# The triangular inverse taken half by half on VectorE, with parts of half 0 placed between the convolution tiles

## The chip, the cores and the metric

One core of one Trainium2 chip. The time is the device time of one execution in microseconds, lower is better. Everything is fp32 or fp32r. Engines: PE (TensorE), DVE (VectorE), ACT (ScalarE), POOL (GpSimd), SP (SyncE, which issues nearly all DMAs here).

## The reference

Input x is 8 x 256 x 128. A gated feed-forward layer with ternary weights, then an attention layer, then the feed-forward layer again, each with a layer norm ahead and a residual. The attention layer, cut to what matters here (H = 4 heads of 32 channels, chunks of 32 tokens, 8 chunks for each of 8 batches):

```python
q, k, v = silu(dwconv(hs @ Wq)), silu(dwconv(hs @ Wk)), silu(dwconv(hs @ Wv))   # 4 taps
beta = sigmoid(hs @ Wb)
q, k = l2norm(q), l2norm(k); v = v * beta; kb = k * beta        # in chunks of 32
attn = where(strict, -(kb @ k.T), 0)
T = inv(eye(32) - attn)                                          # 256 matrices of 32 x 32
u, w = T @ v, T @ kb
# scan over the 8 chunks:
local = where(incl, q_i @ k_i.T, 0); u_i = u - w @ S
o_i = q_i @ S + local @ u_i;         S = S + k_i.T @ u_i
paths = [fir_3(v), fir_15(v), fir_64(v), delta_path, v]          # causal FIR filters of 3, 15, 64 taps
stats = mean, mean square, mean |.|, norm of each path, token and head
logits = gelu([hs, stats] @ gW1 + gb1) @ gW2 + gb2; probs = softmax(...)
o = rmsnorm(sum_p probs_p * paths_p) @ Wo
```

## The kernel before

The list STEPS (L27 to L103) gives one order of steps. PE, ACT and DVE each walk the same list and each carries out its own share of every step, in that order; POOL and SP have short programs of their own. PSUM is two rings of four banks, ps_a (evicted by ACT) and ps_d (evicted by DVE), and the order in the list is the order in each ring. Each engine executes strictly in order, so an instruction that waits holds back everything behind it on its engine.

The 2048 tokens are four tiles of 512 (two batches each). Half 0 is tiles 0 and 1 (batches 0 to 3), half 1 is tiles 2 and 3. The steps of the attention layer that the change touches, in their order before (att_steps, L65 to L99):

- qkv t (PE L806): the four projections of tile t with the convolution's taps folded into the weights, 39 matmuls of 128x512. ACT evicts them (L595, L598, L600) and squares q and k (L603). mean t and var t (L773, L777; ACT L528, L531, L534; DVE L965 to L971, L1067, L1069) are the layer norm of a later tile.
- sumsq t: sums of squares per head (PE L812), reciprocal roots on ACT (L608, L610), then the normalised q, k and k times beta on DVE (L1120 to L1133). Its last instruction signals dve_nrm.
- gram i (half i): for each head, 64 matmuls of 32x32 by 32x64 (PE L836), an ACT copy (L566), a DVE product with a mask (L1139).
- inverse (DVE L1143 to L1164): two transposes bring both halves' matrices to one matrix per partition and half (L1144), 31 steps of forward substitution work on both halves together, each a product (L1154) and a subtraction (L1157) on [128, 2, k, j+1] elements with k = 31 - j, and two transposes bring the result back (L1160). ACT's numbers() (L466 to L475, four small activations and two table loads) stands at this step in ACT's order.
- token 0 to 11: transposes of k, v, kb (PE L826), evicted by ACT (L620). window 0 to 15: transposes of 96-token windows of v (PE L823), evicted by ACT into vt (L614) with the window as outer loop, a destination stride of 64 elements.
- fir 0 to 15: the FIR filters as Toeplitz products (PE L850, 32 records each), evicted by ACT (L627). Their matrices come in four groups of which SBUF holds two; SP loads groups 2 and 3 (L360) when fir 3 and fir 7 are through. yy 0 to 3 (PE L862, ACT L631) need the inverse.
- turn4 (DVE L1163): two transposes of v. Statistics q = 0 to 9: sq q on ACT (L486, a square of 1024 elements), and r1, r2, r3 on DVE (L1201, L1203, L1207, a reduction of 1024 elements each; r3 reads the square). sums(q) is the three together. aq b (PE L872; DVE L1172, L1174) and bo b (PE L872; ACT L635) prepare the recurrence.
- first and rec n (PE L884; DVE L1183, L1187): the recurrence over 8 chunks of half 0, with yy 4 to 7, aq 4 to 7 and reductions between its steps, then turn (L1213), gate and logit (PE L893, L895, L902), and half 1's recurrence beside the softmax and the mixing.
- SP waits for logit 1 before it loads the second feed-forward layer's weights; ACT rounds them (L648).

## Time and profile before

| | |
|---|---|
| median of three executions | 457.12 us (455.99 to 472.33) |
| the profiled execution | 456.23 us, its span 454.5 us |
| busy share of the span | PE 83%, DVE 68%, ACT 63%, POOL 2% |
| mean granted TensorE clock | 0.902 |

The span runs from the first to the last instruction; 1.7 us of the device time lie around it. The busy share is a mean over stages with different limits, so the stage from the first convolution tile (115.6 us) to the statistics of half 0 (turn 0 at 280.4 us) is read by itself, through the chain of waits and the engines' timelines.

### The profile page before, as it was taken

How to read it: one execution, taken by the hardware profiler on the slowest of the kernel's cores; microseconds unless marked ns; L12 is line 12 of the kernel's file. 1: busy time of each engine (PE TensorE's matmuls, PEld its weight loads, DVE VectorE, ACT ScalarE, POOL GpSimd, SP SyncE). 2: the span in 40 equal slices, each digit the busy share in tenths (PEclk: the TensorE clock that was granted, in tenths of full speed). 3: DMA queues.
4: the chain of work that ended last, by engine and by line, in shares of the span. 5: the costliest groups of instructions: out<-in, count | busy, mean ns of one | idle time of the engine just before them, and what ended most of it. 6: DMA issues, size and time to landing. Idle time of an engine off the chain costs nothing.

```text
span 454.5 us, 9702 instructions
## 1 busy us (share of the span) xinstructions
PE 377.9 (83%) x4132; PEld 279.5 (61%) x4132; DVE 307.1 (68%) x461; ACT 288.2 (63%) x434; POOL 9.1 (2%) x38
## 2 busy tenths in 40 slices
PE   5599999999988976977996668936689696978996
PEld 3377776678865746855775567522256575646885
DVE  2796779547124558699979869587867696658533
ACT  4788948888267672796554317337278739457973
POOL 4000000000000010000000000000000000000000
PEclk9899999999999995698997675877689988989999
DMA  8900009200000000000700000070000000001001
GB/s 285 300 1 2 2 1 269 57 1 1 1 1 0 1 0 4 3 0 3 209 6 4 4 4 4 1 247 8 0 1 1 1 1 2 0 1 48 3 1 46
DMA packets 13428, 17.38 MB, mean 38 GB/s; under 512 B 832, under 2 KB 9024, under 8 KB 13376
## 3 DMA queue, kind: packets, MB, share of 16 engines
q1 hardware_dynamic: 13232, 16.58, 11.7%
q8 instruction: 44, 0.72, 0.7%
q14 instruction: 8, 0.07, 0.0%
q10 hardware_dynamic: 144, 0.01, 0.0%
HBM read 15.55 MB, written 1.05 MB: 37 GB/s over the span
## 4 chain that ended last, share of the span: by engine, by line
PE 48%; DVE 25%; ACT 16%; issue 4%; DMA 4%; SPq 1%; DVEq 0%; ACTq 0%
PE ps_a L708 11%; PE ps_a L709 11%; PE ps_a L806 4%; PE ps_a L850 4%; ACT arena L614 3%; DMA w_in<-in_w 2%; PE ps_a L895 2%; PE ps_a L862 2%; PE ps_d L773 2%; PE ps_a L893 2%; DVE acts L1084 2%; DVE arena L971 2%; PE ps_d L709 2%; PE ps_d L708 2%; DVE arena L965 2%
## 5 line engine op out<-in xcount | busy, mean ns | idle before, releaser
L708 PE MATMUL ps_a<-acts,w_f 128*128 128x512 f32 x256 | 103.7, 405 | 9.1 <-ACT acts L582 8.5
L709 PE MATMUL ps_a<-acts,w_f 128*128 128x512 f32 x256 | 101.7, 397 | 0.0
L708 PEld LDWEIGHTS ps_a<-acts,w_f 128*128 128x128 f32 x256 | 49.2, 192 | 22.6 <-ACT acts L582 10.2
L709 PEld LDWEIGHTS ps_a<-acts,w_f 128*128 128x128 f32 x256 | 49.2, 192 | 10.8 <-issue 0.7
L582 ACT ACTIVATE acts<-ps_a,vec 128x512 fp32r<-128x512 f32 x64 | 44.6, 697 | 0.0
L1103 DVE TENSOR_TENSOR acts<-gbuf,acts 128x512 fp32r<-128x512 f32 x32 | 21.6, 690 | 24.9 <-ACT acts L582 24.9
L806 PE MATMUL ps_a<-xnp,conv_w 128*128 128x512 f32 x156 | 38.3, 403 | 0.0
L965 DVE SCALAR_TENSOR_TENSOR arena<-ps_d,arena 128x512 f32<-128x512 f32 x16 | 11.0, 687 | 38.9 <-ACT arena L534 29.4
L1103 DVE TENSOR_TENSOR acts<-ghbuf,acts 128x512 fp32r<-128x512 f32 x32 | 21.2, 689 | 20.8 <-ACT acts L582 20.8
L806 PEld LDWEIGHTS ps_a<-xnp,conv_w 128*128 128x128 f32 x156 | 29.3, 188 | 8.3 <-issue 1.4
L579 ACT ACTIVATE gbuf<-ps_a,vec 128x512 f32<-128x512 f32 x32 | 22.3, 697 | 10.3 <-PE ps_a L709 10.0
L850 PE MATMUL ps_a<-toep,arena 96*32 96x96 f32 x512 | 23.7, 355 | 3.9 <-ACT arena L614 2.8
L579 ACT ACTIVATE ghbuf<-ps_a,vec 128x512 f32<-128x512 f32 x32 | 22.4, 699 | 7.2 <-PE ps_a L709 7.1
L486 ACT ACTIVATE arena<-arena 128x1024 f32<-128x1024 f32 x10 | 10.3, 1052 | 22.8 <-DVE arena L1190 15.1
L850 PEld LDWEIGHTS ps_a<-toep,arena 96*32 96x32 f32 x512 | 18.8, 131 | 7.4 <-ACT arena L614 3.1
L708 PE MATMUL ps_a<-xn,w_f 128*128 128x512 f32 x32 | 15.2, 475 | 7.9 <-DVE ln L966 5.2
L627 ACT ACTIVATE arena<-ps_a 128x384 f32<-128x384 f32 x16 | 13.4, 839 | 13.1 <-PE ps_a L850 13.1
L884 PE MATMUL ps_d<-arena 32*32 32x64 f32 x448 | 11.1, 240 | 9.2 <-DVE arena L1187 4.8
L836 PE MATMUL ps_d<-arena 32*32 32x64 f32 x512 | 12.6, 289 | 6.5 <-DVE arena L966 5.8
L1079 DVE SCALAR_TENSOR_TENSOR hbuf<-ps_d,vec,gbuf 128x512 f32<-128x512 f32 x16 | 11.6, 748 | 8.4 <-ACT gbuf L550 5.1
L1157 DVE TENSOR_TENSOR arena<-arena 128x62 f32<-128x62 f32 (+15 forms) x31 | 16.4, 527 | 1.1
L1154 DVE TENSOR_TENSOR arena<-arena 128x62 f32<-128x62 f32 (+15 forms) x31 | 16.3, 527 | 1.1
...
## 6 DMA issues: line engine op xcount, KB each, us to landing
...
```

The lines of the kernel that those rows point to most:

```text
L579: e.activation(gbuf[f][:, gi % 4], src[:, :], ACT.Gelu, scale=sc).then_inc(S["act_step"], 1)
L582: e.activation(acts[f][:, j % 3, 0, m], src[:, :], ACT.Gelu, scale=sc).then_inc(S["act_a"], 1)
L614: e.activation(vt[0:WIN, :, i // 8, 4 * (i % 8):4 * (i % 8) + 4].rearrange("p c w -> p w c"), bank[0:WIN, :].rearrange("p (w c) -> p w c", ...
L627: e.activation(dst, bank[:, 0:384].rearrange("p (c t f) -> p c t f", c=4, t=DH), ACT.Copy).then_inc(S["act_a"], 1)
L708: e.matmul(bank, w, hi, start=start, stop=False)
L709: return e.matmul(bank, w, lo, start=False, stop=stop)
L806: last = e.matmul(bank, conv_w[:, hw, ww], xnp[:, hx, 2 * i:2 * i + 2, o:o + L], start=n == 0, stop=n == len(todo) - 1)
L850: last = e.matmul(bank[32 * h:32 * h + 32, WIN * c4:WIN * c4 + WIN], vt[0:WIN, DH * h + 8 * grp + dl, i // 2 % 2, :], toep[0:WIN, grp % 2, ...
L965: own(e.scalar_tensor_tensor(out=half_y2, in0=bank, scalar=eps, in1=half_y2, op0=ALU.add, op1=ALU.mult))
L1103: e.tensor_tensor(acts[f][:, j % 3, 1, m], gbuf[f][:, (KT * j + m) % 4], acts[f][:, j % 3, 0, m].bitcast(F32), ALU.subtract).then_inc(S["d ...
L1154: own(e.tensor_tensor(prod, lmat[:, :, j + 1:DH, j:j + 1].to_broadcast(shape), tinv[:, :, j:j + 1, 0:j + 1].to_broadcast(shape), ALU.mult))
L1157: own(e.tensor_tensor(sub, sub, prod, ALU.subtract))
```

## The change

- The inverse is split. Each half has its own matrices lmat and tinv; substitute(g, first, last) does steps first to last of half g with the same two instructions on [128, k, j+1]. Half 0's steps 0 to 10 stand between sumsq 2 and sumsq 3, steps 11 to 14 one behind each head of gram 1, the rest behind gram 1. Half 1's steps stand in four pieces: 0 to 15 ahead of turn4, 16 to 21 and 22 to 30 among the statistics of half 0, and its last transpose just ahead of first 0.
- gram 0 stands between qkv 2 and sumsq 2. Windows 0 to 7 stand two and two behind the convolution tiles, half 0's FIR steps behind sumsq 3, between gram 1 and the tokens. The FIR goes half by half, so that groups 0 and 1 of its matrices are loaded a second time (SP, eight more DMAs).
- sumsq t stands behind tile t, no longer behind tile t + 1, for t = 0 and 1.
- The windows are evicted with four windows innermost (both sides in the order channel, window), and the FIR results in the order filter, token, channel.
- numbers() is moved on ACT to the entry of the attention layer. sums(4) moves ahead of first 0; the order of the statistics changes, so that three reductions fewer stand behind turn 0 and three more ahead of first 0.
- Buffers are placed anew. The number of PE and ACT instructions of the stage is the same but for the order; DVE has 62 more.

The diff, cut to its core:

```diff
+SPLIT = 11
...
+FIR_ORDER = (0, 1, 4, 5, 8, 9, 12, 13, 10, 11, 14, 15, 2, 3, 6, 7)
...
-    for t in range(NT):
-        s.append(("qkv", 2, t))
-        if t + 2 < NT:
-            s += [("mean", 2, t + 2), ("var", 2, t + 2)]
-        if t:
-            s.append(("sumsq", 2, t - 1))
-    s += [("sumsq", 2, NT - 1), ("gram", 2, 0), ("gram", 2, 1), ("inverse", 2, 0)]
-    s += [("token", 2, i) for i in range(12)]
-    s += [("window", 2, i) for i in range(16)]
-    s += [("fir", 2, i) for i in range(12)]
+    for t in range(2):
+        s += [("qkv", 2, t), ("mean", 2, t + 2), ("window", 2, 2 * t), ("window", 2, 2 * t + 1),
+              ("var", 2, t + 2), ("sumsq", 2, t)]
+    s += [("qkv", 2, 2), ("gram", 2, 0), ("lmat", 2, 0), ("window", 2, 4), ("window", 2, 5), ("sumsq", 2, 2),
+          ("qkv", 2, 3), ("solve", 2, 0), ("window", 2, 6), ("window", 2, 7), ("sumsq", 2, 3)]
+    fir = [("fir", 2, i) for i in FIR_ORDER]
+    s += fir[0:4] + [("gram", 2, 1), ("lmat", 2, 1), ("solve", 2, 2), ("xt", 2, 0)]
+    s += [("token", 2, i) for i in (0, 1, 4, 5, 8, 9)] + fir[4:6]
+    s += [("token", 2, i) for i in (2, 3, 6, 7, 10, 11)] + fir[6:8]
+    s += [("window", 2, i) for i in range(8, 16)]
     for k in range(4):
-        s += [("yy", 2, k), ("fir", 2, 12 + k)]
-    s += [("turn4", 2, 0), ("sq", 2, 0), ("turn4", 2, 1), ("sq", 2, 1)] + sums(0) + [("sq", 2, 2)] + sums(1)
-    s += [("sq", 2, 3), ("aq", 2, 0), ("r1", 2, 2), ("aq", 2, 1), ("r2", 2, 2), ("r3", 2, 2), ("sq", 2, 4),
-          ("aq", 2, 2), ("r1", 2, 3), ("aq", 2, 3), ("r2", 2, 3), ("r3", 2, 3)]
-    s += [("bo", 2, b) for b in range(4)] + [("sq", 2, 5)]
+        s += [("yy", 2, k), fir[8 + k]]
+    s += [("solve", 2, 3), ("solve", 2, 4), ("turn4", 2, 0), ("sq", 2, 0), ("turn4", 2, 1), ("sq", 2, 1)] + sums(0) + [("sq", 2, 2)] + sums(1)
+    s += [("sq", 2, 3), ("aq", 2, 0), fir[12], ("solve", 2, 5), ("r1", 2, 2), ("aq", 2, 1), fir[13], ("solve", 2, 6), ("r2", 2, 2), ("r3", 2, 2), ("sq", 2, 4),
+          ("aq", 2, 2), fir[14], ("r1", 2, 3), ("aq", 2, 3), fir[15], ("r2", 2, 3), ("r3", 2, 3)]
+    s += [("bo", 2, b) for b in range(4)] + [("sq", 2, 5)] + sums(4) + [("sq", 2, 6), ("xt", 2, 1)]
     ahead = [("yy", 2, k) for k in range(4, 8)] + [("aq", 2, k) for k in range(4, 8)]
-    between = {1: [("r1", 2, 4)], 2: [("r2", 2, 4)], 3: [("r3", 2, 4)], 4: [("numbers", 2, 0)] ,
-               5: [("r1", 2, 5)], 6: [("r2", 2, 5)], 7: []}
+    between = {1: [("r1", 2, 5)], 2: [("r2", 2, 5)], 3: [("r3", 2, 5)], 4: [("numbers", 2, 0)],
+               5: [("r1", 2, 6)], 6: [("r2", 2, 6)], 7: [("r3", 2, 6)]}
     s += [("first", 2, 0)]
     for n in range(1, NCH):
         s += [("rec", 2, n), ahead[n - 1]] + between[n]
-    s += [("turn3", 2, 0), ("sq", 2, 6), ("aq", 2, 7), ("bo", 2, 4), ("bo", 2, 5), ("bo", 2, 6), ("r3", 2, 5)]
-    s += sums(6) + [("turn", 2, 0), ("bo", 2, 7), ("sq", 2, 7), ("sq", 2, 8), ("first", 2, 1),
-                       ("gate", 2, 0), ("gate", 2, 1)]
+    s += [("turn3", 2, 0), ("sq", 2, 7), ("aq", 2, 7), ("bo", 2, 4), ("bo", 2, 5), ("bo", 2, 6)]
+    s += sums(7) + [("turn", 2, 0), ("bo", 2, 7), ("sq", 2, 8), ("first", 2, 1), ("gate", 2, 0), ("gate", 2, 1)]
     half = [None] + [("rec", 2, NCH + n) for n in range(1, NCH)]
-    s += sums(7) + [("r1", 2, 8), ("r2", 2, 8), half[1], ("logit", 2, 0), ("r3", 2, 8), half[2], ("logit", 2, 1),
-                    ("lturn", 2, 0), half[3], ("soft", 2, 0), ("round", 2, 0), half[4], ("prob", 2, 0), ("mul", 2, 0), half[5], ("addmix", 2, 0), ("mul", 2, 1), ("add", 2, 1), ("osq", 2, 1),
-          half[6], ("rms", 2, 0), half[7], ("scale", 2, 0), ("turn3", 2, 1), ("sq", 2, 9), ("wo", 2, 0), ("wo", 2, 1)]
+    s += sums(8) + [half[1], ("logit", 2, 0), half[2], ("logit", 2, 1),
+                    ("lturn", 2, 0), half[3], ("soft", 2, 0), ("round", 2, 0), half[4], ("prob", 2, 0), ("mul", 2, 0),
+                    half[5], ("addmix", 2, 0), ("mul", 2, 1), ("add", 2, 1), ("osq", 2, 1),
+                    half[6], ("rms", 2, 0), half[7], ("scale", 2, 0), ("turn3", 2, 1), ("sq", 2, 9), ("wo", 2, 0), ("wo", 2, 1)]
     s += sums(9)
...
-STATS = ((4, 0), (0, 0), (1, 0), (2, 0), (4, 1), (0, 1), (3, 0), (1, 1), (2, 1), (3, 1))
-LAST_STAT = (6, 9)
+STATS = ((4, 0), (0, 0), (1, 0), (2, 0), (4, 1), (0, 1), (1, 1), (3, 0), (2, 1), (3, 1))
+LAST_STAT = (7, 9)
...
-          vk=0, bo=0, yu=4096, lmat=4096, tinv=6144, tmp=38400, ssb=22016, alt=8192, vt=14336, aq1=19968, xt=30720, paths=24576,
+          vk=0, bo=0, yu=4096, lmat0=32768, tinv0=33792, lmat1=6144, tinv1=7168, ssb=22016, alt=8192, vt0=24576, vt1=16384, aq1=19968, xt=14336, paths=24576,
...
-        lmat, tinv = at("lmat", G, DH, DH), at("tinv", G, DH, DH)
-        tmp = at("tmp", 512)
-        pall = at("paths", P, G, DH, DH)
+        lmat, tinv = ([at(f"{name}{g}", DH, DH) for g in range(G)] for name in ("lmat", "tinv"))
+        tmp = [at("xt", G, DH * DH)[:, g, 0:256] for g in range(G)]
+        pall = at("paths", G, P, DH, DH)[:, ::-1].rearrange("p g a t c -> p a g t c")
...
-            for grp in (2, 3):
-                e.wait_ge(S["pe_a"], A_AT[("fir", 2, 4 * (grp - 2) + 3)] + 1)
+            for grp, last_use in ((2, 1), (3, 5), (0, 11), (1, 15)):
+                e.wait_ge(S["pe_a"], A_AT[("fir", 2, last_use)] + 1)
...
+            e.wait_ge(S["dve_xn"], VAR_AT[("var", 2, NT - 1)] + 1)
+            own(e.memset(at("tinv0", DH * DH), 0.0))
+            e.memset(at("tinv0", DH * DH)[:, 0:DH * DH:DH + 1], 1.0).then_inc(S["eye_done"], 1)
             e.wait_ge(S["pe_a"], A_AT[("qkv", 2, NT - 1)] + 4)
-            own(e.memset(at("tinv", G * DH * DH), 0.0))
-            e.memset(at("tinv", G, DH * DH)[:, :, 0:DH * DH:DH + 1], 1.0).then_inc(S["eye_done"], 1)
+            own(e.memset(at("tinv1", DH * DH), 0.0))
+            e.memset(at("tinv1", DH * DH)[:, 0:DH * DH:DH + 1], 1.0).then_inc(S["eye_done"], 1)
...
                 if s in ENTRY:
+                    numbers()
...
-                    e.wait_ge(S["dve_nrm"], NT)
+                    e.wait_ge(S["dve_nrm"], NT * (i + 1) // 2)
...
-                        e.activation(vt[0:WIN, :, i // 8, 4 * (i % 8):4 * (i % 8) + 4].rearrange("p c w -> p w c"),
-                                     bank[0:WIN, :].rearrange("p (w c) -> p w c", w=4), ACT.Copy
+                        e.activation(vt[i // 8][0:WIN, :, 4 * (i % 8):4 * (i % 8) + 4],
+                                     bank[0:WIN, :].rearrange("p (w c) -> p c w", w=4), ACT.Copy
...
-                    dst = pall[:, 0:3, i // 2 % 2, :, c:c + 4][:, :, ::-1, :].rearrange("p f t c -> p c t f")
-                    e.activation(dst, bank[:, 0:384].rearrange("p (c t f) -> p c t f", c=4, t=DH), ACT.Copy
+                    dst = pall[:, 0:3, i // 2 % 2, :, c:c + 4][:, :, ::-1, :]
+                    e.activation(dst, bank[:, 0:384].rearrange("p (c t f) -> p f t c", c=4, t=DH), ACT.Copy
...
-                        e.wait_ge(S["act_a"], A_AT[("qkv", 2, NT - 1)] + 3)
+                    if s == ("window", 2, 0):
                         e.wait_ge(S["pad_zero"], 1)
+                    if kind == "window" and i % 4 == 0:
+                        e.wait_ge(S["act_a"], A_AT[("qkv", 2, i // 4)] + 3)
...
-                    grp = i // 4
-                    if i == 0:
-                        e.wait_ge(S["act_a"], A_AT[("window", 2, 15)] + 1)
-                    if i % 4 == 0:
-                        e.wait_ge(S[f"ld_t{grp % 2}"], 64 * (grp // 2 + 1))
+                    grp, half = i // 4, i // 2 % 2
+                    if i == FIR_ORDER[8 * half]:
+                        e.wait_ge(S["act_a"], A_AT[("window", 2, 8 * half + 7)] + 1)
+                    if i % 2 == 0:
+                        e.wait_ge(S[f"ld_t{grp % 2}"], 64 * (3 - grp // 2 if half else 1 + grp // 2))
...
+            def substitute(g, first, last):
+
+                for j in range(first, last):
+                    k = DH - 1 - j
+                    shape = [128, k, j + 1]
+                    sub = tinv[g][:, j + 1:DH, 0:j + 1]
+                    prod = tmp[g][:, 0:k * (j + 1)].rearrange("p (i c) -> p i c", i=k)
+                    settle()
+                    own(e.tensor_tensor(prod, lmat[g][:, j + 1:DH, j:j + 1].to_broadcast(shape),
+                                        tinv[g][:, j:j + 1, 0:j + 1].to_broadcast(shape), ALU.mult))
+                    settle()
+                    own(e.tensor_tensor(sub, sub, prod, ALU.subtract))
+                if last == DH - 1:
+                    settle()
...
+                        if i:
+                            substitute(0, SPLIT + h, SPLIT + h + 1)
+                elif kind == "lmat":
+                    own(e.transpose(lmat[i].rearrange("p i j -> p (i j)"),
+                                    alt[i][:, :, :, 0, :].rearrange("p h n t -> p t (h n)")))
+                elif kind == "solve":
+                    if i == 0:
+                        e.wait_ge(S["eye_done"], 1)
+                        substitute(0, 0, SPLIT)
+                    elif i == 2:
+                        substitute(0, SPLIT + H, DH - 1)
+                    else:
+                        if i == 3:
+                            e.wait_ge(S["eye_done"], 2)
+                        substitute(1, *((0, 8), (8, 16), (16, 22), (22, DH - 1))[i - 3])
+                elif kind == "xt":
+                    e.transpose(xt[:, i].rearrange("p h n t -> p t (h n)"), tinv[i].rearrange("p i j -> p (i j)")
+                                ).then_inc(S["inv_done"], 1)
...
-                        e.wait_ge(S["act_a"], A_AT[("fir", 2, 15)] + 1)
+                        e.wait_ge(S["act_a"], A_AT[("fir", 2, FIR_ORDER[8 * g + 7])] + 1)
```

## Rows read from the trace of the kernel before

**Rows 1.** The page: busy time of the engines, and their share of the chain.
```profile
PE 377.9 (83%) x4132; PEld 279.5 (61%) x4132; DVE 307.1 (68%) x461; ACT 288.2 (63%) x434; POOL 9.1 (2%) x38
PE 48%; DVE 25%; ACT 16%; issue 4%; DMA 4%; SPq 1%; DVEq 0%; ACTq 0%
```
**Rows 2.** The chain of waits, 178 to 256 us: start, length, engine and line.
```profile
177.48 0.70 DVE arena L1133
...
186.08 1.28 ACT L472
...
189.19 5.86 ACT arena L620 x12
195.05 14.25 ACT arena L614 x16
...
217.18 4.68 DMA toep<-in_fir
...
244.33 0.29 DVE arena L1172
```
**Rows 3.** DVE's timeline: start, length, line, output<-input, count, idle time before.
```profile
225.08 4.07 DVE L1160 STREAM_TRANSPOSE arena<-arena 128x1024 f32<-128x1024 f32 x2
229.02 4.04 DVE L1163 STREAM_TRANSPOSE arena<-arena 128x1024 f32<-128x1024 f32 x2
239.73 1.22 DVE L1207 TENSOR_REDUCE arena<-arena 128x32 f32<-128x1024 f32 x1 [4.45 <-ACT arena L486]
240.87 1.21 DVE L1201 TENSOR_REDUCE arena<-arena 128x32 f32<-128x1024 f32 x1
253.38 0.30 DVE L1178 STREAM_TRANSPOSE arena<-arena 128x128 f32<-128x128 f32 x1
280.36 1.95 DVE L1213 STREAM_TRANSPOSE arena<-arena 128x1024 f32<-128x1024 f32 x1 [0.61 <-ACT arena L643]
291.98 0.42 DVE L1183 TENSOR_TENSOR arena<-arena,ps_d 128x256 f32<-128x256 f32 x1 [3.75 <-PE ps_d L884]
```
**Rows 4.** DVE's timeline: one head of gram 1, two sizes of the inverse's instructions.
```profile
182.91 0.42 DVE L1139 TENSOR_TENSOR arena<-ps_d,mask 128x256 f32<-128x256 f32 x1 [0.83 <-ACT arena L566]
192.26 0.39 DVE L1154 TENSOR_TENSOR arena<-arena 128x224 f32<-128x224 f32 x1
192.69 0.40 DVE L1157 TENSOR_TENSOR arena<-arena 128x224 f32<-128x224 f32 x1
207.00 0.69 DVE L1154 TENSOR_TENSOR arena<-arena 128x512 f32<-128x512 f32 x1
207.73 0.69 DVE L1157 TENSOR_TENSOR arena<-arena 128x512 f32<-128x512 f32 x1
```
**Rows 5.** Busy time by stretch: length, PE, PEld, DVE, ACT, POOL, then PE's granted clock.
```profile
170.00:175.00 5.00, 1.81 (x85) 1.46 (x80) 4.86 (x10) 1.24 (x3) 0.00 (x0) 0.66 0.02 5
253.38:280.36 26.98, 20.07 (x934) 18.45 (x938) 20.11 (x42) 8.12 (x13) 0.00 (x0) 0.69 0.02 4
```
**Rows 6.** PE's timeline: a convolution tile, a norm, gram 0's first head.
```profile
115.58 9.29 PE L806 MATMUL ps_a<-xnp,conv_w 128*128 128x512 f32 x39
127.08 1.13 PE L777 MATMUL ps_d<-arena,mean_w 128*128 128x512 f32 x2 [1.35 <-ACT arena L528]
169.02 1.09 PE L836 MATMUL ps_d<-arena 32*32 32x64 f32 x64 [2.61 <-DVE arena L966]
```
**Rows 7.** Timelines of ACT and DVE in the convolution stage.
```profile
118.66 1.28 ACT L600 ACT_TABLE_LOAD   x1 [5.23 <-PE ps_a L806]
142.15 0.69 DVE L965 SCALAR_TENSOR_TENSOR arena<-ps_d,arena 128x512 f32<-128x512 f32 x1 [9.11 <-ACT arena L534]
145.26 0.42 DVE L1120 TENSOR_SCALAR arena<-arena 128x512 f32<-128x512 f32 x1
150.44 0.69 DVE L1133 TENSOR_TENSOR arena<-arena 128x512 f32<-128x512 f32 x1
```
**Rows 8.** The chain of waits behind turn 0: the gate's first and last matmuls.
```profile
282.36 1.65 PE ps_a L893 x3
...
289.77 0.69 PE ps_a L893 x3
```

More of the change, by code:

```diff
@@ L216, in program @@
         acts.append(sb("acts1", [128, 3, 2, KT, TILE], F32R, c3))
-        sb("small1", [128, AO["vt"] - AO["small"]], F32, c3)
+        sb("small1", [128, AO["xt"] - AO["small"]], F32, c3)
         w_f.append(sb("w_f1", [128, 5632], F32R, c3))
@@ L240, in ln_bufs @@
             if f == 1:
-                v = at("paths", P, 2, 2, TILE)
-                return {k: v[:, 1 + i, 0] for i, k in enumerate(("xc", "sq", "y", "u"))}
+                v = at("paths", G, P, 2, TILE)
+                return {k: v[:, 1, 1 + i] for i, k in enumerate(("xc", "sq", "y", "u"))}
             v = {0: ln_0, 2: at("ln", 8, TILE)}[f]
@@ L253, in program @@
         vpad = at("vpad", B, HIST + L)
-        vt = at("vt", 128, G, 32)
-        alt = at("alt", G, H, NCH, 3, DH)
+        vt = [at(f"vt{g}", 128, 32) for g in range(G)]
+        alt = [at("alt", G, H, NCH, 3, DH)[:, 1 - g] for g in range(G)]
         xt = at("xt", G, H, NCH, DH)
@@ L562, in _ @@
                 elif kind == "gram":
[L563 removed]
+                    e.wait_ge(S["dve_nrm"], NT * (i + 1) // 2)
                     for h in range(H):
                         e.wait_ge(S["pe_d"], dd + h + 1)
[L566 removed]
+                        e.activation(alt[i][:, h, :, 0], ps_d[:, (dd + h) % NRING].rearrange(
                             "p (n a t) -> p n a t", n=NCH, a=2)[:, :, 0], ACT.Copy).then_inc(S["act_l"], 1)
[L568 to L569 removed]
                 elif kind in ("hid1", "hid2"):
```

38 lines of the change are left out of this document (7 added, 31 removed).

## The prediction

> **What bounds the kernel now.** I read the page first: PE is busy 83% of the span and holds 48% of the chain, DVE 68% and 25% [rows 1]. These are means over stages, so the second view is the chain of waits, cut at the stage that the change rearranges. From 178.2 us, where DVE ends the last normalisation, it goes over gram to ACT's numbers(), the token evictions (5.86 us), the window evictions (14.25 us for 16, 0.89 each), FIR products with a wait for their matrices (4.68 us), and reaches DVE at 239.7 us [rows 2]. So before 239.7 us ACT and PE bound the stage, and the change takes their work away from there.
>
> The third view, DVE's own timeline, qualifies this. The inverse's 62 instructions run from 190.26 to 225.08 us, then two pairs of transposes, and DVE idles only 4.45 us before 239.73 us [rows 3]. From there it works without a break up to the first step of the recurrence at 253.38 us. **So a second chain, on DVE alone, lies 4.45 us below the first.** All the time taken from ACT and PE beyond this is slack, and what DVE is given in addition counts.
>
> **The price of halving.** An instruction on 224 elements has a pitch of 0.43 us, one on 512 of 0.73 [rows 4]: about 0.20 us fixed and 1.024 ns an element. One half's 31 steps have 5456 elements (the sum of (31 - j)(j + 1)), twice. Together before: 62 x 0.20 + 21824 x 0.001024 = 34.7 us, against 34.8 in the trace. A half alone: 12.4 + 11.2 = 23.6 us; two halves 47.1. DVE has 12.3 us more to do. By the same formula, pieces of half 0: steps 0 to 10 7.7 us, 11 to 14 3.6, 15 to 30 12.25. Of half 1: 0 to 15 12.25, 16 to 21 5.4, 22 to 30 6.0.
>
> **The convolution stage in the new order.** A tile costs PE 9.2 us, a norm's matmul 0.86, a sumsq 1.72 (a pair of matmuls of the same size), two windows 1.3, a gram head 1.09 at the full clock [rows 6]. numbers() falls into ACT's 5.23 us of idle time ahead of the first eviction [rows 7] and costs nothing: its 3.3 us fit; if they didn't, the first evictions would be late by the excess, and PE has four banks. Windows 0 to 3 partly fill PE's wait of 1.35 us before each norm. In order: qkv 0 115.6 to 124.8, then mean, windows, var and sumsq 0 to 129.7; qkv 1 to 138.9; the same again to 143.9; qkv 2 to 153.1. gram 0 needs sumsq 1's DVE part. ACT does two window evictions (1.8 us) ahead of tile 3's norm, plus a table load and two activations, to 145.7; DVE 3.1 us for the norm and 5.8 for sumsq 1 [rows 7], to 154.6. PE waits 1.5 us, then gram 0 to 159.1, windows 4 and 5 and sumsq 2 to 162.1, qkv 3 to 171.3 (before: 161.8). ACT evicts windows 4 and 5, loads its table (1.28 us), and gives the first root at 164.1; DVE finishes sumsq 2 at 168.8 and steps 0 to 10 at 176.5. sumsq 3's DVE part then takes 5.8 us, to 182.3; ACT's root for it is there at 177.4, so both bind about alike. **The stage ends at 182.3 us instead of 178.2, +4.1**, with gram 0, eight windows and eleven steps done in it. (gram's mask products and the first transposition, 3.6 us, lie in DVE's wait for ACT.)
>
> **From there to the recurrence, all on DVE.** First head of gram 1 ready 1.6 us after 182.3; four times a mask product and a step, 0.42 + 0.91 [rows 4], 5.3; transposition 1.9; steps 15 to 30 12.25; xt 0 2.05; half 1's steps 0 to 15 12.25; turn4 3.85; six reductions at 1.13 [rows 3] 6.75; aq 0 to 3 at 0.6 [rows 2] 2.4; steps 16 to 30 11.3; six reductions 6.75; sums(4), moved here, 3.4; xt 1 1.95. Sum 71.8 us, so first 0 starts at **254.1 us against 253.38, +0.7**. Before it was 75.2 us from 178.2: the idle 4.45, the four gram heads and one transposition are saved, the fixed costs and sums(4) added.
>
> What must stay below DVE for this. Half 0's FIR starts at about 175 and needs window 7; groups 2 and 3 of its matrices, asked for behind fir 1 and fir 5, are there 6.3 us later, before their use near 190. Windows 8 to 15 are evicted by about 208, yy and FIR end near 218, DVE wants them at 228. The reloads of groups 0 and 1 (eight DMAs on SP, queued behind waits for fir 11 and fir 15) land by about 225; SP has nothing else before the weights behind logit 1. The closest cover: ACT's fir evictions 14 and 15 now wait behind sq 4, so behind the third r3; bo 2 needs their bank. From that r3, ACT 1.0 + 0.85, two bo 4.4 and an eviction 0.6 make about 7.5 us, while DVE has 9.5 us before first 0. Slack 2.
>
> **The new eviction order** has no row. Windows cost 0.89 us now with every element 256 bytes from the last; tokens, in runs of 32, cost 0.49 each [rows 2]. Now they write runs of four and read PSUM at a stride. Bounds: 0.49, and 0.89 plus the same penalty again, 1.3. I take 0.89, the row of the same instruction. Windows stand twice on the path (before tile 3's norm, before sumsq 2's root); at 0.49 the stage ends up to 1.6 us sooner, at 1.3 up to 1.6 later. The FIR evictions are under cover either way.
>
> The Trainium skill (SBUF — State Buffer, "Door 1: The DMA port swizzle") says that accesses within 16 bytes go at full speed in SBUF and a crossing costs, and that PSUM has lines of 8 bytes. By its first half four fp32 windows side by side would be written near the contiguous price and the sum would be 1.6 us less; by its second half the strided PSUM read gives this back. No row here shows either for ACT.
>
> **Behind first 0.** Nine reductions lie between first 0 and turn 0 in both orders, so the 26.98 us stay. Behind turn 0 three reductions are gone (3.4 us), but there DVE idles 3.75 us waiting for PE [rows 3], so I count them at nothing; the cover is PE's gates. The sum on the profiled execution is 456.23 + 0.7 = 456.9, 0.2 below the shown median. **Predicted: 457.0 us.**
>
> **Rivals.**
> 1. Faster by the recurrence (0.22). In the 26.98 us DVE is busy 20.11, and PE's granted clock is 0.69 [rows 5]. With the first gate's three matmuls in 1.65 us at the low level (1.2 GHz) and the last's in 0.69 at the high one [rows 8], a PE that arrives at the higher clock gives 2 to 3 us back, a tighter loop 1 to 2, cheap evictions 1.6. It gives about 451.5. Against it: PE has even less to do ahead of the recurrence than before, which speaks for the same low clock.
> 2. Slower by PE's clock in the convolution stage (0.15). PE was busy 1.81 us in 170 to 175 and its clock fell to 0.66 there [rows 5], behind waits of 2.6 us [rows 6]. The new order makes PE wait 1.5 us and then run small matmuls just ahead of qkv 3. If the clock falls there, qkv 3 takes up to twice 9.2 us, and as sumsq 3 has only about 0.2 us of slack every microsecond counts from the first. Half of it gives +4.6: 461.6; the whole 466.
> 3. Slower by bo (0.08): fir 14 and 15's evictions hold bo 2 for more than the 2 us of slack, or the reload is late; first 0 comes 2 to 4 us later, 460.
> 4. The change doesn't do what it says: half 0's early steps only push sumsq 3 back. By the sum they delay it by 0.2 us, for ACT's roots are no sooner; if ACT were quicker (cheap evictions) up to 1.6 of their 7.7 us would be exposed. It cancels part of rival 1 and stays within 456 to 458.
>
> **Numbers.** The forecast with rival 4 has 0.55 (454.5 to 459.5), rivals 1 to 3 have 0.22, 0.15 and 0.08. For 8 in 10 the range takes in most of rival 1 and rivals 2 and 3 up to half a tile at the low clock: 450.5 to 463. No change can be told within 2%, 9.1 us: faster than 448 needs all of rival 1 and more (0.07), slower than 466.3 a whole tile at the low clock (0.07).
>
> **What would show it.** L1154 and L1157 as 124 instructions of 47 us together with no idle time; the last L1133 near 182; first 0 (L1178) near 254; ACT waiting for DVE rather than DVE for ACT between 205 and 254; r3 0 with no wait before it. It is wrong if PE's clock is below 1 before 170, if DVE waits for L1178's bo, or if the pitch at small sizes isn't 0.20 plus 1.024 ns an element.

## The result and the profile after

The changed kernel takes **462.73 us** (median; 462.54 to 463.2), against 456.79 for the kernel before it on the same chip: ratio **1.0144 [1.0125, 1.0164]**. It is 1.4% slower, where practically no change was forecast (457.0); the time lies at the upper end of the range, and the mechanism that put it there is not among the rivals. One execution of the kernel before ran slow (472.33 us), and the ratios leave it out. Every ratio in this document is to the kernel before on the same chip; its median there lay between 455.5 and 456.8 us, so times of different experiments are compared by their ratios. The profiled execution took 463.2 us with a span of 461.5, 7.0 us more than the span before.

The page of the kernel after, parts 1, 4 and 5 (to compare with [rows 1]):

```profile
PE 377.8 (82%) x4132; PEld 281.2 (61%) x4132; DVE 315.9 (68%) x523; ACT 277.6 (60%) x434; POOL 9.6 (2%) x40
...
PE 50%; DVE 28%; ACT 10%; issue 8%; DMA 3%; SPq 0%; DVEq 0%; ACTq 0%
...
L1060 DVE TENSOR_TENSOR arena<-arena 128x31 f32<-128x31 f32 (+15 forms) x62 | 21.3, 343 | 2.1
L1057 DVE TENSOR_TENSOR arena<-arena 128x31 f32<-128x31 f32 (+15 forms) x62 | 21.1, 341 | 1.9
```

The inverse is 124 instructions, 62 of each of two kinds. DVE's shares say little more. The place of the loss shows only in the chain of waits of the kernel after (start, length, what), which answers to [rows 2]:

```profile
153.73 2.03 PE ps_d L844 x142
155.76 1.64 issue
157.40 2.68 PE ps_d L844 x105
160.09 1.87 PE ps_a L831 x8
161.96 2.99 PE ps_d L818 x4
164.95 9.12 PE ps_a L812 x39
...
183.49 0.70 DVE arena L1156
...
184.24 4.24 PE ps_d L844 x210
188.48 4.33 issue
192.81 1.53 PE ps_d L844 x46
...
194.37 0.39 ACT arena L574
...
194.78 0.42 DVE arena L1162
```

L844 is gram (L836 before), L818 sumsq, L812 a convolution tile, L831 a window, L1156 the last product of a norm. Both grams contain an "issue" piece: PE waits for no other engine there, yet does not run. In gram 1 this lasts 4.33 us, exactly in front of the last 46 of its 256 matmuls.

DVE's timeline of the kernel after, the lines that answer to [rows 3] and [rows 4] (L1162 mask product, L1167 first transposition, L1180 xt, L1184 turn4, L1197 first 0, L1232 turn 0):

```profile
177.21 0.40 DVE L1060 TENSOR_TENSOR arena<-arena 128x231 f32<-128x231 f32 x1
...
179.38 0.69 DVE L973 SCALAR_TENSOR_TENSOR arena<-ps_d,arena 128x512 f32<-128x512 f32 x1 [0.70 <-ACT arena L616]
...
194.78 0.42 DVE L1162 TENSOR_TENSOR arena<-ps_d,mask 128x256 f32<-128x256 f32 x1 [4.84 <-ACT arena L574]
...
195.91 1.95 DVE L1167 STREAM_TRANSPOSE arena<-arena 128x1024 f32<-128x1024 f32 x1
...
210.03 2.01 DVE L1180 STREAM_TRANSPOSE arena<-arena 128x1024 f32<-128x1024 f32 x1
...
287.68 1.94 DVE L1232 STREAM_TRANSPOSE arena<-arena 128x1024 f32<-128x1024 f32 x1 [0.90 <-ACT arena L649]
...
298.88 0.42 DVE L1202 TENSOR_TENSOR arena<-arena,ps_d 128x256 f32<-128x256 f32 x1 [5.59 <-PE ps_d L892]
```

The 4.45 us of idle time ahead of a reduction [rows 3] are gone; DVE has none from 195.91 us to first 0, at 259.85. In their place it waits 4.84 us for the last head of gram 1.

The sum of the forecast, set against this trace:

```
stretch                           forecast    measured    off by
to the end of sumsq 3             182.3       184.2       +1.9
from there to the transposition     6.9        11.7       +4.8
transposition to first 0           64.9        63.94      -1.0
first 0 to turn 0                  26.98       27.83      +0.85
turn 0 to the end                 174.14      173.82      -0.3
                                                  sum     +6.3
```

With the 0.7 that the forecast itself added, these are the 7.0 us of span.

### The profile page after: what moved, and what is told of

Same layout as the page of the kernel before. It is cut to its first block, busy times and chain, and to the rows that moved or that the text cites. A ratio compares the mean times of both kernels' runs of the same rounds, so it can differ in the third digit from the quotient of the medians.

```text
span 461.5 us, 9781 instructions
## 1 busy us (share of the span) xinstructions
PE 377.8 (82%) x4132; PEld 281.2 (61%) x4132; DVE 315.9 (68%) x523; ACT 277.6 (60%) x434; POOL 9.6 (2%) x40
## 4 chain that ended last, share of the span: by engine, by line
PE 50%; DVE 28%; ACT 10%; issue 8%; DMA 3%; SPq 0%; DVEq 0%; ACTq 0%
PE ps_a L714 11%; PE ps_a L715 10%; PE ps_a L812 6%; DVE arena L1060 4%; DVE arena L1057 4%; PE ps_d L844 2%; DMA w_in<-in_w 2%; PE ps_d L714 2%; PE ps_d L715 2%; PE ps_d L779 2%; PE ps_a L903 2%; PE ps_a L901 2%; DVE acts L1107 2%; PE ps_a L880 2%; DVE hbuf L1102 1%
## 5 line engine op out<-in xcount | busy, mean ns | idle before, releaser
L812 PE MATMUL ps_a<-xnp,conv_w 128*128 128x512 f32 x156 | 38.3, 403 | 0.0
L812 PEld LDWEIGHTS ps_a<-xnp,conv_w 128*128 128x128 f32 x156 | 29.4, 188 | 8.5 <-issue 1.7
L858 PE MATMUL ps_a<-toep,arena 96*32 96x96 f32 x512 | 25.2, 355 | 1.3 <-issue 1.3
L880 PE MATMUL ps_a<-arena 32*32 32x64 f32 x512 | 11.8, 285 | 15.0 <-ACT arena L633 13.6
L1060 DVE TENSOR_TENSOR arena<-arena 128x31 f32<-128x31 f32 (+15 forms) x62 | 21.3, 343 | 2.1
L1057 DVE TENSOR_TENSOR arena<-arena 128x31 f32<-128x31 f32 (+15 forms) x62 | 21.1, 341 | 1.9
L892 PE MATMUL ps_d<-arena 32*32 32x64 f32 x448 | 11.8, 247 | 12.0 <-issue 7.0
L880 PEld LDWEIGHTS ps_a<-arena 32*32 32x32 f32 x512 | 10.7, 147 | 16.0 <-ACT arena L633 14.1
L892 PEld LDWEIGHTS ps_d<-arena 32*32 32x32 f32 x448 | 9.3, 124 | 16.1 <-issue 10.4
```

What stands on the lines that cost most here:

```text
L812: last = e.matmul(bank, conv_w[:, hw, ww], xnp[:, hx, 2 * i:2 * i + 2, o:o + L], start=n == 0, stop=n == len(todo) - 1)
L858: last = e.matmul(bank[32 * h:32 * h + 32, WIN * c4:WIN * c4 + WIN], vt[half][0:WIN, DH * h + 8 * grp + dl, :], toep[0:WIN, grp % 2, h, :, ...
L880: last = e.matmul(bank[c, 64 * n:64 * n + 64], yu[r, g, h, n, o:o + DH], alt[g][r, h, n, 1:3].rearrange("p x c -> p (x c)"), start=True, s ...
L892: last = e.matmul(bank[r, 64 * b:64 * b + 64].rearrange("p (x t) -> p x t", x=2), s_sb[r, g, b], aqs[g][r, b, n], start=True, stop=True)
L1057: own(e.tensor_tensor(prod, lmat[g][:, j + 1:DH, j:j + 1].to_broadcast(shape), tinv[g][:, j:j + 1, 0:j + 1].to_broadcast(shape), ALU.mult))
L1060: own(e.tensor_tensor(sub, sub, prod, ALU.subtract))
```

## The experiments

**Theory A:** in gram 1, PE waits for instructions to arrive from memory, and the FIR loads that the change asked for earlier (on SP, behind fir 1 and fir 5, which now run ahead of gram 1) fill the DMA engines just then. **Rival:** the 124 small DVE instructions, or the slower clock, are the cost.

The DMA queues of the kernel after, in 188 to 190 and then in 190 to 191 us (packets, MB, share of 16 engines), the last stretch before PE resumes:

```profile
q1 hardware_dynamic: 188, 0.49, 106.6%
...
q1 hardware_dynamic: 63, 0.15, 61.7%
q8 instruction: 1, 0.02, 7.9%
```

The loads fill the engines from 183 us on (93% and more), and the queue "instruction" shows no packet from 183 to 190. One comes through in the microsecond in which the loads run out, and the matmuls go on at 192.81.

### The loads put behind gram 1

```diff
             load_toep(e, 1)
+            e.wait_ge(S["pe_d"], D_AT[("gram", 2, 1)] + H)
             for grp, last_use in ((2, 1), (3, 5), (0, 11), (1, 15)):
```

> The changed kernel with one wait more: SP issues the loads of FIR groups 2 and 3 only when PE has ended gram 1. In the changed kernel PE stands still for 4.33 us in gram 1's last head while these loads fill the DMA engines. Theory A (PE's instructions come over the same DMA engines and queue behind the loads): the standstill shrinks to the 1.6 to 2.0 us of the other gaps marked as issue, the stage behind it comes 2.3 to 2.7 us sooner, and the time falls by 2 to 2.7 us to about 460.3 us, if FIR 8 doesn't then wait for its matrices on the path. Theory B (PE runs out of instructions in dense small matmuls whatever the DMA engines do): the gap stays above 4 us and the time within 0.5 us of 462.7. Theory C (the gap is a wait for DVE or ACT that the profile doesn't name): no change either.

Measured (run e1): 458.71 us, ratio 1.0065 [1.0037, 1.0093] to the kernel before. That is 0.8% below the kernel after: more than half of the loss is back. PE's timeline of this kernel:

```profile
183.54 2.78 PE L845 MATMUL ps_d<-arena 32*32 32x64 f32 x210 [1.24 <-DVE arena L1157]
188.00 1.50 PE L845 MATMUL ps_d<-arena 32*32 32x64 f32 x46 [1.69 <-issue]
...
197.28 3.02 PE L859 MATMUL ps_a<-toep,arena 96*32 96x96 f32 x64 [2.88 <-DMA toep<-in_fir]
```

The standstill stays at the same matmul, the 211th, but is 1.69 us instead of 4.33. Its instruction packet comes in 185 to 186 us, with no other transfer in flight. FIR now waits 2.88 us for its matrices, and this costs nothing: DVE has no idle time from the transposition (191.10) to first 0 (255.04). The gain, 3.6 us by the ratios, is larger than the 2 to 2.7 expected, because the stretch behaved as a whole: gram 1 from first to last matmul lasted 5.96 us here and 10.07 in the kernel after, where the first 210 also took 4.24 us instead of 2.78.

### The same loads beside gram 1, in the kernel before

```diff
+            e.wait_ge(S["ld_t0"], 64)
+            e.wait_ge(S["ld_t1"], 64)
+            e.wait_ge(S["pe_d"], D_AT[("gram", 2, 1)])
+            load_toep(e, 0)
+            load_toep(e, 1)
...
-                        e.wait_ge(S[f"ld_t{grp % 2}"], 64 * (grp // 2 + 1))
+                        e.wait_ge(S[f"ld_t{grp % 2}"], 64 * (grp // 2 + 2))
```

> The kernel before, with the FIR matrices of groups 0 and 1 loaded a second time while gram 1 runs (SP issues the eight DMAs when PE has ended gram 0; the same data, 2.3 MB). Nobody waits for these loads: the first FIR step comes 23 us later. Theory A (instructions queue behind loads): PE's standstills in gram 1 and the tokens behind it grow by 2 to 3 us in sum, gram 1 is on the path of ACT and DVE alike, and the time rises by 1.5 to 4 us, to 458 to 461 us. Theory B (no link between loads and standstills): within 0.5 us of the kernel before.

Measured (run e2): 457.75 us, ratio 1.0054 [1.0029, 1.0080], 2.5 us slower. PE's timeline of this kernel:

```profile
177.99 5.64 PE L841 MATMUL ps_d<-arena 32*32 32x64 f32 x244 [0.56 <-DVE arena L1144]
186.17 0.64 PE L841 MATMUL ps_d<-arena 32*32 32x64 f32 x12 [2.55 <-issue]
```

In the kernel before, the 256 are one piece:

```profile
179.19 6.35 PE L836 MATMUL ps_d<-arena 32*32 32x64 f32 x256 [0.56 <-DVE arena L1139]
```

With nothing else changed, eight loads beside a gram lengthen it from 6.35 to 8.82 us. The rival is out for this part: neither halving nor a new order is in this kernel, and the first 244 matmuls run as fast as before (5.64 us against 5.63 in its chain of waits). So it is shown, from both sides, that loads beside a gram lengthen it. That the matmuls wait for their instructions is an inference, from the fixed place of the standstill and the times of the instruction packets; no run took the two apart. The packet need not wait for the loads to run out: here it comes through at 183 to 184 us, with the engines still full of loads (103%), and PE resumes at 186.17.

### Gram 0 back behind the tiles

```diff
-    s += [("qkv", 2, 2), ("gram", 2, 0), ("lmat", 2, 0), ("window", 2, 4), ("window", 2, 5), ("sumsq", 2, 2),
-          ("qkv", 2, 3), ("solve", 2, 0), ("window", 2, 6), ("window", 2, 7), ("sumsq", 2, 3)]
+    s += [("qkv", 2, 2), ("window", 2, 4), ("window", 2, 5), ("sumsq", 2, 2),
+          ("qkv", 2, 3), ("window", 2, 6), ("window", 2, 7), ("sumsq", 2, 3), ("gram", 2, 0), ("lmat", 2, 0), ("solve", 2, 0)]
```

> The changed kernel with gram 0, its transposition and steps 0 to 10 placed behind sumsq 3, the windows left between the tiles. Theory (gram 0 between the tiles pays for itself by cover): qkv 3 starts 8 us sooner, sumsq 3 ends near 176.5 instead of 184.1, but the transposition and eleven steps (9.5 us) stand uncovered on DVE, so gram 1 begins to be read 2 to 4 us later and the time rises by 2 to 4 us over 462.7. Rival (the cost of gram 0 between the tiles, a standstill of 1.6 us and a matmul clock of 0.56 behind it, is larger than its cover): the time falls by 1 to 3 us.

Measured (run e4): 457.08 us, ratio 1.0042 [1.0015, 1.0069]. I had expected it slower than the kernel after; it is 1.0% faster, and my price for this step fell. sumsq 3 ends at 175.4 us instead of 184.2, and steps 0 to 10 now lie in the wait for gram 1. Its PE and DVE timelines:

```profile
181.64 2.78 PE L844 MATMUL ps_d<-arena 32*32 32x64 f32 x210
188.34 1.50 PE L844 MATMUL ps_d<-arena 32*32 32x64 f32 x46 [3.92 <-issue]
```

```profile
190.32 0.42 DVE L1162 TENSOR_TENSOR arena<-ps_d,mask 128x256 f32<-128x256 f32 x1 [0.36 <-ACT arena L574]
```

The standstill is still 3.92 us, but DVE waits only 0.36: there are eleven steps to do meanwhile.

### Both at once

```diff
+            e.wait_ge(S["pe_d"], D_AT[("gram", 2, 1)] + H)
```

(the line of the first experiment, in the kernel of the one before this)

> The run e4 (gram 0, its transposition and steps 0 to 10 behind the tiles) with the loads of groups 2 and 3 behind gram 1 as in e1. In e4 the standstill of PE in gram 1 still lasts 3.92 us, but DVE is at work on steps 0 to 10 and idles only 0.36 us for it. Theory (the standstill costs only where DVE waits for gram 1): the standstill falls to about 1.7 us and the time falls by 0 to 1 us from 457.1, against 4.0 us in e1. Rival (the loads cost time by themselves): it falls by 2.5 to 4 us as there.

Measured (run e11): 457.65 us, ratio 1.0043 [1.0023, 1.0064], no different from 1.0042. Gram 1 shrinks from 8.20 to 5.11 us:

```profile
181.52 2.78 PE L845 MATMUL ps_d<-arena 32*32 32x64 f32 x210
185.76 0.87 PE L845 MATMUL ps_d<-arena 32*32 32x64 f32 x46 [1.47 <-issue]
```

and the time does not move. So the standstill is paid only where DVE has nothing to do beside it, and the two repairs are two ways to the same 4 us, not a sum. The same numbers price gram 0's place by itself: with the loads out of the way in both, 1.0065 with it between the tiles and 1.0043 with it behind them, 0.2%, which the intervals don't tell apart.

### Without the late steps of half 1

```diff
-                        substitute(1, *((0, 8), (8, 16), (16, 22), (22, DH - 1))[i - 3])
+                        substitute(1, *((0, 8), (8, 16), (16, 16), (16, 16))[i - 3])
                 elif kind == "xt":
+                    settle()
```

> The changed kernel without steps 16 to 30 of half 1's inverse (30 DVE instructions, 11.1 us in its trace; this part of the computation is left out). If DVE alone bounds the stretch from 196 us to the recurrence, the time falls by 10 to 11.1 us, to about 452 us. If PE's or ACT's work (bo 2 and bo 3, held back by the evictions behind the fourth square, or the second load of the matrices) lies close below, it falls by less: first 0 had 4.1 us behind bo 3's eviction, which shifts with the removed instructions, so a fall of under 8 us would mean such a chain.

Measured (run e5): 450.82 us, ratio 0.9895 [0.9867, 0.9923], 2.5% (11.4 us) below the kernel after. The steps left out take 5.2 + 5.9 us there. Its first 0, on DVE's timeline:

```profile
246.26 0.28 DVE L1198 STREAM_TRANSPOSE arena<-arena 128x128 f32<-128x128 f32 x1
```

13.6 us sooner than 259.85. 2.5 of it was there at the transposition (193.43 us instead of 195.91), and 11.1 us come from the stretch, which is what the steps took. Nothing took their place: DVE bounds the stretch up to first 0, as the forecast had it.

### The light ACT work in the kernel before

numbers() at the entry and both eviction orders, without halving:

```diff
-                        e.activation(vt[0:WIN, :, i // 8, 4 * (i % 8):4 * (i % 8) + 4].rearrange("p c w -> p w c"),
-                                     bank[0:WIN, :].rearrange("p (w c) -> p w c", w=4), ACT.Copy
+                        e.activation(vt[0:WIN, :, i // 8, 4 * (i % 8):4 * (i % 8) + 4],
+                                     bank[0:WIN, :].rearrange("p (w c) -> p c w", w=4), ACT.Copy
...
-                    dst = pall[:, 0:3, i // 2 % 2, :, c:c + 4][:, :, ::-1, :].rearrange("p f t c -> p c t f")
-                    e.activation(dst, bank[:, 0:384].rearrange("p (c t f) -> p c t f", c=4, t=DH), ACT.Copy
+                    dst = pall[:, 0:3, i // 2 % 2, :, c:c + 4][:, :, ::-1, :]
+                    e.activation(dst, bank[:, 0:384].rearrange("p (c t f) -> p f t c", c=4, t=DH), ACT.Copy
```

> The kernel before with ACT's share of the change alone: numbers() at the entry of the attention layer, windows and FIR results evicted in the new element order; order of steps, joint inverse and buffers as before. My theory (a DVE chain lies 4.45 us below the ACT and PE chain): ACT's chain gets shorter by 3.1 (numbers), 16 x 0.39 = 6.2 (windows) and more (FIR), the FIR's end by about 9, DVE's idle time of 4.45 us before the third reduction goes to about 0, and nothing beyond it: 456.8 - 4.4 = 452.4 us. Rival: the ACT and PE chain was all that counted, 447 to 448 us. Rival: what is gained is given back in the recurrence, 456 to 457 us.

Measured (run e3): 456.2 us, ratio 1.0020 [0.9988, 1.0051]: no gain, and my expectation fell. Its PE timeline tells why,

```profile
214.06 5.87 PE L849 MATMUL ps_a<-toep,arena 96*32 96x96 f32 x128 [1.16 <-DMA toep<-in_fir]
226.24 1.93 PE L861 MATMUL ps_a<-arena 32*32 32x64 f32 x64 [6.31 <-DVE arena L1159]
```

and DVE's:

```profile
239.49 1.22 DVE L1206 TENSOR_REDUCE arena<-arena 128x32 f32<-128x1024 f32 x1 [5.53 <-ACT arena L486]
```

PE is through fir 11 at 219.9 us, 7.8 sooner than before, and then waits 6.31 us for the inverse's transposition, with fir 12 to 15 queued behind yy 0 to 3. The interleave of yy and FIR then takes its old time, DVE again waits 5.53 us for ACT's sq 0 (4.45 before), and all is as it was. **The two chains of the forecast were one:** inverse, transposition, yy and FIR in turn on PE, ACT's sq 0, DVE. The 4.45 us were no slack of an independent chain; they were FIR's last four groups, done where DVE could see them.

### FIR wholly ahead of yy, inverse not halved

```diff
-    s += [("fir", 2, i) for i in range(12)]
-    for k in range(4):
-        s += [("yy", 2, k), ("fir", 2, 12 + k)]
+    s += [("fir", 2, i) for i in range(16)]
+    s += [("yy", 2, k) for k in range(4)]
```

(on top of the previous experiment)

> The kernel before with ACT's lighter evictions and numbers() moved (as in the run e3), and all sixteen FIR steps ahead of yy 0. In e3 PE reached yy 0 early and waited 6.31 us for the inverse with four FIR steps queued behind it, so ACT's first square still came at 237.9 and DVE idled 5.53 us. Theory (the order on PE, inverse to yy to FIR to square to r3, holds DVE): with the FIR ahead, this idle time goes to nearly 0 and the time falls by 4.5 to 5.5 us, to about 451 us. Rival (something else holds the square): no change from e3, 456 us. Rival (given back in the recurrence): 454 to 456 us.

Measured (run e7): **450.59 us, ratio 0.9886 [0.9855, 0.9916]**, 1.1% faster than the kernel before, as expected, and the fastest complete kernel of this study. Its PE and DVE timelines:

```profile
226.62 3.77 PE L860 MATMUL ps_a<-arena 32*32 32x64 f32 x255 [1.48 <-DVE arena L1158]
```

```profile
233.99 1.22 DVE L1205 TENSOR_REDUCE arena<-arena 128x32 f32<-128x1024 f32 x1
...
247.63 0.32 DVE L1176 STREAM_TRANSPOSE arena<-arena 128x128 f32<-128x128 f32 x1
```

The FIR products lie beside the inverse, PE idles 1.48 us before yy, the first r3 (L1205) waits for nothing, and first 0 comes at 247.63 instead of 253.38. Of the 5.75 us, 4.45 are that idle time, 0.4 were there before the inverse ended, and the four transpositions behind the inverse took 0.8 less. No step of the inverse was halved for them.

### One joint inverse in the new order

All 31 steps over both halves behind gram 1, both transpositions right behind; the rest as in the kernel after:

```diff
-    s += fir[0:4] + [("gram", 2, 1), ("lmat", 2, 1), ("solve", 2, 2), ("xt", 2, 0)]
+    s += fir[0:4] + [("gram", 2, 1), ("lmat", 2, 1), ("solve", 2, 0), ("xt", 2, 0), ("xt", 2, 1)]
...
-                    shape = [128, k, j + 1]
+                    shape = [128, G, k, j + 1]
```

> The changed kernel with the inverse in one piece again: all 31 steps on both halves together behind gram 1, both transposes right behind, everything else in the changed order. 62 DVE instructions fewer; DVE's total falls by 12.3 us, but the 7.5 us of steps between the tiles and the 3.6 us between gram 1's heads were mostly under cover. Theory (the fixed 0.2 us of each added instruction, less what the cover hides): the convolution stage ends 1 to 2 us sooner (179 to 183), gram 1's path about 1.5 us shorter, then 34.8 + 4 us instead of 12.1 + 2 + 12 + 11.1 + 2, so the recurrence starts 1 to 4 us sooner and the time is 459 to 462 us. If halving itself made the change slow, it should fall to 456.8 us or below. If the small pieces are all hidden, it stays at 462.7 or rises.

Measured (run e6): 466.86 us, ratio 1.026 [1.0187, 1.0334] (four executions), slower still than the kernel after; I had expected 459 to 462, so this expectation fell too. Its PE and DVE timelines:

```profile
191.09 1.50 PE L844 MATMUL ps_d<-arena 32*32 32x64 f32 x46 [5.90 <-issue]
```

```profile
193.05 0.42 DVE L1165 TENSOR_TENSOR arena<-ps_d,mask 128x256 f32<-128x256 f32 x1 [7.13 <-ACT arena L574]
...
247.13 1.22 DVE L1220 TENSOR_REDUCE arena<-arena 128x32 f32<-128x1024 f32 x1 [7.31 <-ACT arena L493]
```

There are two waits. No steps of half 0 fill the standstill in gram 1 (7.13 us; PE's last 46 matmuls waited 5.90); yet the last head's product comes at 193.05, 1.7 us sooner than in the kernel after, as gram 0 and sumsq 2 took less. And yy, with FIR between, waits for the whole inverse (7.31 us): this one makes the kernel the slower of the two, for from the last head's product to first 0 it takes 71.8 us, the kernel after 65.1. So what halving bought was work done inside the first wait and the removal of the second, and each has another remedy.

### The joint inverse with both remedies

FIR ahead of yy (the four FIR steps among the statistics too), and the loads behind gram 1:

```diff
-    for k in range(4):
-        s += [("yy", 2, k), fir[8 + k]]
+    s += fir[8:16] + [("yy", 2, k) for k in range(4)]
...
+            e.wait_ge(S["pe_d"], D_AT[("gram", 2, 1)] + H)
```

> The run e6 (changed order, joint inverse) with all of half 1's FIR steps ahead of yy 0, and with the loads of groups 2 and 3 behind gram 1 as in e1. In e6 DVE idled 7.3 us behind the inverse, for FIR results that PE held back behind yy 0, and 7.1 us in gram 1. Theory (halving pays only because yy and FIR were interleaved, and DVE's sum decides otherwise): both idle times shrink, by about 7 and 4 us, and the time is 454 to 457 us, below the run e1 (458.7), which is the same with the inverse halved. If halving has a merit of its own, it stays above e1.

Measured (run e9): 455.84 us, ratio 1.0005 [0.9986, 1.0025], against 1.0065 for the halved kernel with late loads (e1): 0.6%, 2.7 us. That is not the price of halving: first 0 comes almost at the same time in the two profiled executions, this kernel's line first,

```profile
254.80 0.30 DVE L1191 STREAM_TRANSPOSE arena<-arena 128x128 f32<-128x128 f32 x1
```

```profile
255.04 0.27 DVE L1198 STREAM_TRANSPOSE arena<-arena 128x128 f32<-128x128 f32 x1
```

and the other 2.4 us lie behind it, where both kernels have the same steps; no run says why. Then gram 0 behind the tiles as well, and gram 1 ahead of half 0's FIR:

```diff
-    s += [("qkv", 2, 2), ("gram", 2, 0), ("lmat", 2, 0), ("window", 2, 4), ("window", 2, 5), ("sumsq", 2, 2),
-          ("qkv", 2, 3), ("window", 2, 6), ("window", 2, 7), ("sumsq", 2, 3)]
-    s += fir[0:4] + [("gram", 2, 1), ("lmat", 2, 1), ("solve", 2, 0), ("xt", 2, 0), ("xt", 2, 1)]
+    s += [("qkv", 2, 2), ("window", 2, 4), ("window", 2, 5), ("sumsq", 2, 2),
+          ("qkv", 2, 3), ("window", 2, 6), ("window", 2, 7), ("sumsq", 2, 3), ("gram", 2, 0), ("lmat", 2, 0)]
+    s += [("gram", 2, 1)] + fir[0:4] + [("lmat", 2, 1), ("solve", 2, 0), ("xt", 2, 0), ("xt", 2, 1)]
```

> The run e9 (joint inverse, half 1's FIR ahead of yy 0, loads behind gram 1) with gram 0 and its transposition behind the tiles and half 0's first four FIR steps behind gram 1. No step of the inverse is between the tiles or between the heads. sumsq 3 should end near 175.5 instead of 184, gram 1's last head near 182, the inverse begin near 185 instead of 192.4: 7 us sooner, and the time 448.5 to 450 us, at or below the run e7 (450.6). If the interleaving in the convolution stage had been worth its cost, it stays above 455.

Measured (run e10): 452.52 us, ratio 0.993 [0.9903, 0.9958], against 1.0043 for the halved kernel with both changes (e11): 1.1%, 5 us. Of these, 4.1 are there at first 0 (250.71 against 254.78). It is faster than the kernel before, but 2.5 to 4 us short of the expectation. Its PE and DVE timelines:

```profile
218.59 3.05 PE L858 MATMUL ps_a<-toep,arena 96*32 96x96 f32 x64 [5.01 <-DMA toep<-in_fir]
...
225.16 1.98 PE L870 MATMUL ps_a<-arena 32*32 32x64 f32 x124
```

```profile
233.68 1.22 DVE L1220 TENSOR_REDUCE arena<-arena 128x32 f32<-128x1024 f32 x1 [2.93 <-ACT arena L493]
```

Now the last FIR matrices are late (5.01 us), yy stands behind FIR, and DVE waits 2.93 us: the same in-order queue as before, from its other end. That is the size of what is missing, though I did not run a kernel with earlier loads to prove it.

## Why the prediction was wrong

The forecast was no change, and the kernel lost 1.4%. The step that failed is the term for gram 1, "four times a mask product and a step, 0.42 + 0.91": it let DVE be the bound there, took PE's heads at their full pace, and put what the moved loads do to PE at nothing. Measured, the stretch took 11.7 us instead of 6.9: PE stood still for 4.33 us beside these loads, and with the loads behind gram 1 (e1) it took 7.6. That 462.73 us still lies inside the range is luck: the upper end was set for rival 2, half a tile at the low clock, and that did not happen.

**What bounds the kernel (wrong).** The chain of waits was read rightly up to 239.7 us, but the second chain "4.45 us below the first" does not exist. ACT's load there is not the bound: taking it away gives 1.0020 [0.9988, 1.0051]. The idle 4.45 us come from yy and FIR sharing PE's queue, and moving four list entries, on top of the lighter ACT work, recovers them and more (the four entries moved alone were not run). This failure did not move the sum, for the 4.45 us are gone in the kernel after as forecast; it misjudged what it takes to win them.

**The price of halving (right).** Steps 0 to 10 took 7.5 us (7.7 forecast), 15 to 30 of half 0 12.1 (12.25), 0 to 15 of half 1 12.0 (12.25), 16 to 21 5.2 (5.4), 22 to 30 5.9 (6.0): 1 to 3% below 0.20 us plus 1.024 ns an element. That DVE bounds the whole stretch is shown by the run without the late steps. Against a joint inverse with FIR first the halves cost 0.2 us up to first 0 (e1 and e9), and 4.1 with gram 0 behind the tiles (e11 and e10). These pairs differ also in FIR's place, the second also in that of gram 1, so the figures are for the pair of orders, not for the 12.3 us of work alone. A halved kernel with FIR ahead of yy was not run; as DVE has no idle time in e1 from the transposition to first 0, I would expect nothing from it.

**The convolution stage, 182.3 us forecast, 184.2 measured (failed by 1.9, and in its premise).** numbers() was hidden, the windows cheaper than assumed, and steps 0 to 10 ended at 177.53, and DVE, after two short products, still waited 0.70 us for ACT's root (179.38), so they did not push sumsq 3 back: rival 4 is out. But from gram 0's start (153.73) to the end of the windows PE took 8.2 us against 5.7: a standstill of 1.64 us and matmuls at a lower clock. sumsq 2 then took 2.99 instead of 1.72. Busy time of the kernel after by stretch (length, PE, PEld, DVE, ACT, POOL, PE's granted clock, DMA share, GB/s):

```profile
155.00:160.00 5.00, 3.36 (x171) 3.07 (x161) 1.27 (x3) 1.11 (x3) 0.00 (x0) 0.76 0.01 3
160.00:165.00 5.00, 5.00 (x17) 3.10 (x14) 3.29 (x4) 3.92 (x6) 0.00 (x0) 0.56 0.01 3
165.00:170.00 5.00, 5.00 (x23) 4.01 (x22) 4.61 (x9) 3.34 (x5) 0.00 (x0) 1.00 0.01 2
...
185.00:190.00 5.00, 3.48 (x170) 3.24 (x162) 3.49 (x9) 1.15 (x3) 0.00 (x0) 0.50 1.05 246
```

Rival 2 came true in part: the clock fell to 0.56, but it was back at 1.00 for tile 3, which took its 9.12 us. The premise failed too: gram 0 between the tiles was thought to be work done early. Taken out again, with the same halves, it gives 4.6 us back while the loads stand beside gram 1 (1.0042 against 1.0144), and 0.2%, nothing that can be told, once they are behind it (1.0043 against 1.0065). So it is not the place between the tiles that costs the 4.6 us; the steps that it lets DVE do early are wanted more in the wait for gram 1.

**From sumsq 3 to the transposition (failed, +4.8, the largest).** Here stands the step that failed: with "0.42 + 0.91" four times DVE was the bound, and gram cost 1.09 us a head. The prediction counted the moved FIR loads by when they land and asked who needs them. It did not ask what else uses the DMA engines at that moment. Gram 1 from first to last matmul:

```
without loads in flight:  before 6.35   loads behind gram 5.96   both repairs 5.11   joint, FIR first 5.75   last joint 7.09
with loads beside it:     after 10.07   before + loads 8.82      gram 0 behind 8.20  joint inverse 10.19     no late steps 9.51
```

Where a standstill shows, it stands before the same matmul, the 211th in the new order (the 245th in the old), which is a place in the instruction stream and not a point in time. (In the last joint kernel, too: after 339 of 384 matmuls of both grams in one piece, which leaves 45 or 46 of gram 1. The joint kernel with FIR first, whose matmuls ran at a granted clock of 0.50 to 0.60, shows none.) The first 210 at a lower clock (4.24 against 2.78 us) do not decide: the joint inverse in the new order ran them in 2.78 and then stood 5.90 us.

**From the transposition to first 0 (right, -1.0)**, with all covers in place: bo 3 was evicted at 255.7, 4.1 us before first 0, so rival 3 is out.

**The new eviction order (bounds right, value too high).** ACT's timeline of the kernel after:

```profile
207.85 0.49 ACT L633 ACTIVATE arena<-ps_a 128x384 f32<-128x384 f32 x1 [0.92 <-PE ps_a L858]
208.41 4.00 ACT L620 ACTIVATE arena<-ps_a 96x512 f32<-96x512 f32 x8
```

A window costs 0.50 us, not 0.89. By the first half of the section of the Trainium skill that the prediction weighed (SBUF — State Buffer, "Door 1: The DMA port swizzle"), accesses within 16 bytes go at full speed, and the trace agrees: 0.50 us, against 0.49 for the tokens, written in runs of 32 [rows 2]. A penalty for the strided read of PSUM does not show here. In the kernel after it earned nothing there, since DVE bounds the stretch.

**Behind first 0.** 27.83 us at a clock of 0.68 against 26.98 at 0.69 [rows 5]: rival 1 is out, there was no gain. Nor is it a loss that can be told: over the twelve profiled executions this stretch took 26.2 to 27.9 us, and 27.7 to 27.9 in the three experiments on the kernel before, whose steps there are unchanged. The three reductions fewer behind turn 0 were worth nothing, as forecast: DVE waits 5.59 us for PE there, where it waited 3.75.

**Open.** Why the first 210 matmuls of gram 1 ran at the lower clock in the kernel after (and in e9 and e10) and not in e1, e4, e5, e6 and e11; and the differences of some 2 us behind first 0 between profiled executions of kernels with the same steps there.
